# Thirty gathers, sixteen single-row loads, six comparisons and thirty-six matmuls added behind the last group of an edge kernel

## The reference, cut to what matters

```python
h = relu(layernorm(x))
p1 = tanh(h @ pp_W1 + pp_b1) @ pp_W2 + pp_b2
inter = concat([p1[src], p1[dst]], -1)
inter = ((inter @ pi_W1 + pi_b1) @ pi_W2 + pi_b2) @ pi_W3
i1 = einsum('ecb,eb->ec', inter.reshape(E, 64, 8), edge_attr_8)
i1 = tanh(i1 @ ii_W1 + ii_b1) @ ii_W2 + ii_b2
out = x + segment_sum(i1, dst, 6250)
```

## Time and profile before

| | us |
|---|---|
| median of 2 runs | 2029.59 |
| lowest, highest | 2029.33, 2029.85 |
| span of the profiled execution, first to last instruction | 2030.8 |
| granted TensorE clock, mean | 0.937 |
| TensorE busy / DVE / ACT / POOL, share of the span | 87% / 65% / 54% / 74% |

### The profile page before, as it was taken

One profiled execution on the slowest core, in us unless ns is written; L12 is line 12 of the kernel. 1 busy time (PEld: TensorE's weight loads), 2 busy tenths in 40 slices (PEclk: granted clock), 3 DMA queues, 4 the chain that ended last, 5 costly groups with the idle time before them and its releaser, 6 DMA issues.

```text
span 2030.8 us, 54857 instructions
## 1 busy us (share of the span) xinstructions
PE 1771.0 (87%) x19990; PEld 1155.3 (57%) x19990; DVE 1322.5 (65%) x1894; ACT 1100.3 (54%) x2401; POOL 1501.1 (74%) x1582
## 2 busy tenths in 40 slices
PE   7698888888888989888898889998888888888898
PEld 6465555555555555555555555555555555555665
DVE  7676666666666666666666666666656666666665
ACT  5565555555555555555555555555555555555554
POOL 2777777777777777777777777777777777777774
PEclk9799999899999899999999999988989999899999
DMA  5533233232332332323323323323233233222231
GB/s 132 126 68 61 56 60 63 54 61 54 64 61 55 62 60 55 61 55 61 61 56 61 62 57 61 61 56 60 56 60 61 57 61 59 55 58 56 57 74 42
DMA packets 261683, 126.82 MB, mean 62 GB/s; under 512 B 183546, under 2 KB 233705, under 8 KB 261433
## 3 DMA queue, kind: packets, MB, share of 16 engines
q1 hardware_dynamic: 210863, 74.12, 17.1%
q0 software_dynamic: 50048, 51.35, 14.3%
q10 hardware_dynamic: 646, 0.13, 0.0%
HBM read 119.47 MB, written 6.00 MB: 62 GB/s over the span
## 4 chain that ended last, share of the span: by engine, by line
POOL 68%; issue 22%; PE 7%; DMA 1%; DVE 1%; ACT 1%; SPq 1%; DVEq 0%; ACTq 0%; POOLq 0%
POOL u_rows L469 68%; PE bank L1162 3%; PE bank L1145 1%; PE bank L1239 1%; DMA u_rows<-u_tab,src_e 1%; PE bank L1169 0%; PE spread_ps L1154 0%; DMA x_sb<-x 0%; DVE o_sb L796 0%; PE spread_ps L1016 0%; PE bank L1137 0%; ACT loc_rows L571 0%; PE spread_ps L1004 0%; DMA v_tab<-acc_all 0%; SPq L353 0%
## 5 line engine op out<-in xcount | busy, mean ns | idle before, releaser
L469 POOL DMA_INDIRECT u_rows<-u_tab,src_e x1564 | 1494.6, 956 | 508.9 <-issue 475.2
L796 DVE TENSOR_TENSOR o_sb<-st_sb,spread_ps 128x2048 f32<-128x2048 f32 x391 | 894.1, 2287 | 484.4 <-PE spread_ps L1154 472.8
L614 ACT ACTIVATE st_sb<-bank,s_bias 64x256 f32<-64x256 f32 x1564 | 734.3, 470 | 462.5 <-PE bank L1145 446.4
L1162 PE MATMUL bank<-o_sb,g_sb 128*64 128x256 f32 x6256 | 844.3, 417 | 1.0 <-DVE o_sb L796 0.8
L1162 PEld LDWEIGHTS bank<-o_sb,g_sb 128*64 128x64 f32 x6256 | 447.6, 147 | 248.2 <-issue 61.0
L1145 PE MATMUL bank<-ident,u_rows 128*128 128x128 f32 x1564 | 287.0, 308 | 217.9 <-DMA u_rows<-u_tab,src_e 216.8
L1145 PEld LDWEIGHTS bank<-ident,u_rows 128*128 128x128 f32 x1564 | 210.3, 195 | 265.9 <-DMA u_rows<-u_tab,src_e 245.1
L1239 PEld LDWEIGHTS bank<-hot,t_sb 128*65 128x65 f32 x3128 | 222.9, 143 | 158.0 <-issue 155.8
L602 ACT ACTIVATE tt_sb<-bank,z_bias 128x256 f32<-128x256 f32 x391 | 186.1, 476 | 212.7 <-PE bank L1162 212.7
L1239 PE MATMUL bank<-hot,t_sb 128*65 128x42 f32 x3128 | 270.0, 239 | 0.5 <-ACT t_sb L605 0.5
L605 ACT COPY t_sb<-bank 128x256 f32<-128x256 f32 x391 | 146.9, 376 | 218.0 <-PE bank L1169 218.0
(11 more groups left out here) (113 smaller groups left out, 239.6 us busy)
## 6 DMA issues: line engine op xcount, KB each, us to landing
loc_bc<-loc_tab SPq DMA_DIRECT2D x391, 126.0 KB
u_rows<-u_tab,src_e POOLq DMA_INDIRECT x1564
v_win<-v_tab SPq DMA_DIRECT2D x391, 15.8 KB
basis<-edge_attr SPq DMA_DIRECT2D x24, 256.0 KB, 4.3
v_tab<-acc_all SPq DMA_DIRECT2D x6, 336.0 KB
u_tab<-basis SPq DMA_DIRECT2D x6, 224.0 KB
x_sb<-x SPq DMA_DIRECT2D x1, 1120.0 KB
out<-x_sb SPq DMA_DIRECT2D x1, 784.0 KB
```

What stands on the lines that cost most here:

```text
L469: pool.indirect_dma_start(out=u_rows[:, g % UR, j, :], out_offset=None, in_=u_tab[:, :], in_offset=bass.IndirectOffsetOnAxis(ap=src_e[:, g ...
L614: last = nc.scalar.activation(tiles[h * D:(h + 1) * D, j], s_ps[r][part].rearrange("p (q a e) -> p q a e", q=2, a=TILES), ACT.Identity, bi ...
L796: return nc.vector.tensor_tensor(o_sb[:, r, :, :].rearrange("p c (j e) -> p j c e", j=TILES), st_sb[:, r, :].rearrange("p (j e) -> p j e", ...
L1162: last = nc.tensor.matmul(z_ps[h * D:(h + 1) * D, 0:2 * P], g_sb[:, c, :], o_sb[:, r, c, 2 * h * P:(2 * h + 2) * P], start=(c == 0), stop= ...
```

## The change

Behind everything that the fast path did, each engine gets more work. Its results go to buffers that nothing reads for the output. POOL, after the last group's rows are placed, issues 30 more gathers from `u_tab`, three each of 128, 127, 126, 124, 120, 112, 96, 64, 32 and 16 rows, and waits for them. SP and ACT each, behind their stores, wait for these 30 gathers, then read eight indices from `src_e` one after the other, issue for each a load of a single row of `u_tab`, and wait for the eight. DVE, behind its last addition, copies the iota to PSUM and repeats comparisons with that operand (four of the `hot` kind and two of the `hot_t` kind). TensorE, behind `y_late`, waits for DVE and for the gathers and does three times the sum by target, six transposes and six products with the identity. Nothing is removed or moved.

```diff
+    TRIED = (128, 127, 126, 124, 120, 112, 96, 64, 32, 16)
...
@@ SP, fast path
                 store_rest()
+                sp.wait_ge(tried_u, 16 * 3 * len(TRIED))
+                for r in range(8):
+                    row = sp.value_load(src_e[0:1, r:r + 1], min_val=0, max_val=N - 1)
+                    sp.dma_start(u_rows[r:r + 1, 6, 0, :], u_tab[bass.ds(row, 1), :]).then_inc(tried_rows, 16)
+                sp.wait_ge(tried_rows, 16 * 8)
@@ POOL, fast path, behind the loop over the groups
+                pool.wait_ge(s_ready, NG)
+                at = 0
+                for rows in TRIED:
+                    for _ in range(3):
+                        pool.indirect_dma_start(
+                            out=u_rows[0:rows, at // TILES, at % TILES, :], out_offset=None, in_=u_tab[:, :],
+                            in_offset=bass.IndirectOffsetOnAxis(
+                                ap=src_e[0:rows, at:at + 1].bitcast(u32), axis=0),
+                        ).then_inc(tried_u, 16)
+                        at += 1
+                pool.wait_ge(tried_u, 16 * 3 * len(TRIED))
@@ ACT, fast path
                 store_rest()
+                act.wait_ge(tried_u, 16 * 3 * len(TRIED))
+                for r in range(8):
+                    row = act.value_load(src_e[0:1, r:r + 1], min_val=0, max_val=N - 1)
+                    act.dma_start(u_rows[r + 8:r + 9, 6, 0, :], u_tab[bass.ds(row, 1), :]).then_inc(tried_rows_a, 16)
+                act.wait_ge(tried_rows_a, 16 * 8)
@@ DVE, fast path
                 add_late()
+                iota_ps = bank[5][:, 2 * P:2 * P + W]
+                nc.vector.tensor_copy(iota_ps, iota_f[:, 0:W]).then_inc(tried_iota, 1)
+                dve.wait_ge(tried_iota, 1)
+                for g in range(4):
+                    nc.vector.tensor_tensor(
+                        hot[:, g, :, :],
+                        loc_e[:, g * TILES:(g + 1) * TILES].unsqueeze(2).to_broadcast([P, TILES, W]),
+                        iota_ps.unsqueeze(1).to_broadcast([P, TILES, W]), ALU.is_equal)
+                for g in range(2):
+                    nc.vector.tensor_tensor(hot_t[:, g % 2, :], loc_bc[0:3 * W, g, :],
+                                            iota_ps[0:3 * W, 0:1].to_broadcast([3 * W, GE]), ALU.is_equal)
+                dve.drain().then_inc(tried_add, 1)
@@ PE, fast path
                 y_late()
+                pe.wait_ge(tried_add, 1)
+                pe.wait_ge(tried_u, 16 * 3 * len(TRIED))
+                for _ in range(3):
+                    for j in range(TILES):
+                        for h in range(2):
+                            nc.tensor.matmul(bank[4][h * D:(h + 1) * D, 0:W], t_sb[:, h, j, 0:D], hot[:, h, j, :],
+                                             start=(j == 0), stop=(j == TILES - 1))
+                for _ in range(3):
+                    for q in range(2):
+                        nc.tensor.transpose(bank[4][:, q * P:(q + 1) * P],
+                                            u_rows[:, 0, 2 * q:2 * q + 2, :].rearrange("p j k -> p (j k)"), ident[:])
+                for _ in range(3):
+                    for q in range(2):
+                        last = nc.tensor.matmul(bank[4][:, q * P:(q + 1) * P],
+                                                u_rows[:, 0, 2 * q:2 * q + 2, :].rearrange("p j k -> p (j k)"),
+                                                ident[:], start=True, stop=True)
+                last.then_inc(tried_pe, 1)
+                pe.wait_ge(tried_pe, 1)
```

More of the change, by code:

```diff
@@ L259, in program @@
         x_again = sem("x_again")
+        tried_u = sem("tried_u")
+        tried_rows = sem("tried_rows")
+        tried_rows_a = sem("tried_rows_a")
+        tried_add = sem("tried_add")
+        tried_iota = sem("tried_iota")
+        tried_pe = sem("tried_pe")
         stored = sem("stored")
```

## The result

The changed kernel takes 2076.1 us (2075.54 and 2076.66) against 2029.59: a ratio of 1.0226, 95% interval 1.0209 to 1.0243, 46.5 us more. The forecast was 2068.4, 38.8 us more, and "within 2%" had the larger chance. The time is inside the range and beyond the 2% line, on the side of the dear cases.

The account below looks back on a forecast made before the run. One added chain behind the old work was taken as the bound: gathers landed at 2053.2, plus 15.7 for rows and 0.7 way out, 2069.6 against a span of 2030.8; 38.8 us on 2029.6 gave 2068.4 us, range 2061 to 2077.

Parts of the forecast that it names:

- the dear cases: Outcomes slower by more than 2%: Rival 1, Rival 4, most of Rival 2, a sixth of the forecast; together 0.41.
- What bounds the kernel, and where the added chain starts: End of the kernel: gathers released at 2015.60, first starting at 2015.75, then one chain of gathers, row loads, way out.
- Gathers at the full price: POOL's 30 added gathers: steps of 1.25 us, last start at 2052.2, landing 3.5 us later at 2055.7.
- What fewer rows are worth: POOL's smaller gathers: saving between nothing and 7.4 us; a third, 2.5 us, taken, putting the landing at 2053.2.
- Row loads: Register reads and single-row loads behind the gathers: 1.61 us a step on SP, 1.70 on ACT; 15.7 us on ACT.
- What lies beside it: TensorE's added work, 4.4 us or 8.8 at half clock, ends 6.9 us ahead of ACT's rows; DVE's 2.5 us hidden.
- The way out: Program's end behind the last landing: the last 0.7 us of the span, taken as fixed.
- The base: Span difference of 38.8 us added to the median of the runs, 2029.6, giving 2068.4 us.
- Rival 1: Row loads: a register as address makes the issue dear, 0.77 us on SP, 0.94 on ACT; 2071.6 us, chance 0.18.
- Rival 2: POOL's gathers: each costs the full 0.944 us whatever its rows; 2070.9 us, chance 0.15.
- Rival 3: POOL's gathers: time is proportional to their rows; 2063.5 us, chance 0.12.
- Rival 4: Odd row counts run on few DMA engines, POOL held until they have room, losing 5.2 us; 2076.1 us, chance 0.08.

Follow-up runs that it names:

- the run without idle time: Changed kernel with POOL waiting slot by slot instead of for the last group of all, so its 30 gathers follow at once: 2071.78 us, 1.0198 of before.
- 30 full gathers: Changed kernel with all 30 added gathers of 128 rows instead of the ten sizes: 2068.67 us, 1.0182 of before.
- the ten other sizes: Changed kernel with its gather sizes replaced by 122, 125, 121, 61, 31, 17, 100, 113, 97 and 64 rows, three each: 2088.9 us, one execution.
- the kernel with DVE's part alone: Changed kernel with only DVE's copy, six comparisons and the semaphores' declarations left: 2593.5 us against 2589.6 before on that chip, ratio 1.0013.

## Why the prediction was right or wrong

*What bounds the kernel, and where the added chain starts.* Right. The kernel's groups are untouched, the chain is gathers, rows, way out, and the run without idle time took the expected 3 us off it. The release itself came 2.4 us later in this execution. In the other runs that wait for the last placement, on such chips, the first added gather started between 2015.8 and 2021.0, while executions of before spread over 9 us by themselves. The comparison of tails and times above leaves 1 or 2 us of it for the change at the most.

*Gathers at the full price.* Right to 0.1 us, shown with 30 full gathers. Only the landing was mis-sized, 3.5 us for 2.2 to 2.5. The rows that I took had other transfers beside them, which is the likely reason; it wasn't tried.

*What fewer rows are worth.* This is the step that failed, with +8.0 us the largest error. I chose a third of a bound between 0 and 7.4 us less. Measured, the small counts that 16 divides save little: 0.91 for 64 rows, 0.84 for 16 and 0.95 for 112 against 0.944, about 0.6 us for the lot. And the uneven ones cost more: 3 x (2.55 - 0.944) = 4.8 us for 127 rows and 3 x (1.29 - 0.944) = 1.0 for 124, with 0.1 each for 126 and 120. My bounds ended at "saves nothing"; the true value was outside them, +5.5 us above the full price. The sentence of the Trainium skill that I weighed (DMA: Bandwidth & Descriptors, "Anatomy of one DMA — SWDGE (gpsimd) path"), by which many descriptors cost little, holds over 16 engines, where 112 more rows cost 0.1 us, and fails for uneven counts: the cost is 0.013 us for each row of the busiest engine, 1.6 us more for 127 rows.

*Row loads.* The mechanism was right, the size 3.8 us too high. On ACT, which ends the chain, the last issue started 10.6 us behind the landing of the gathers and not 13.1, because the register read was 0.48 us and not 0.77 (on SP 0.49, and the issue 0.26 and not 0.40). From that start to the end it was 2.0 us and not 3.3 (2.6 and 0.7): a single row is back sooner than the loads and stores that I took. I had noted the minimum of 0.464 and what it would save. Why the same read takes 0.77 in the groups wasn't tried.

*What lies beside it.* Hidden, as said, but by less than I wrote. TensorE's products took 5.6 us, where I had priced 4.4 at full clock and 8.8 at half; the pricing was wrong twice. I took 8 entries of the sum by target for all of a round, though a round has 16, and the six placements for 1.5 times instead of 3. Counted rightly, the rows give 7.5 us at full clock. What saved it is that the 48 entries took 2.79 us and not the 4.0 of the earlier trace rows, though at half the clock. The granted clock behind TensorE's 33 us of waiting was 0.50 (the lower level, 1.2 GHz) until 2066, with the products running from 2062.4, and 1.00 (2.4 GHz) from 2067; in the mean of the stretch 0.67:

```profile
2062.00:2069.00 7.00, 5.63 (x66) 5.39 (x66) 0.00 (x0) 0.00 (x0) 0.00 (x0) 0.67 0.01 3
```

The margin to ACT's end was 3.1 us instead of 6.9, because TensorE's way out takes 3.5.

*The way out.* 0.7 us fits where SP or ACT is last, and is wrong as a constant: POOL's drain took 0.55 to 8.1 us behind the added gathers, and TensorE's came 3.4 to 4.0 us behind the added products, 2.0 behind the last ones of before. What sets either wasn't tried. It cost the sum nothing, as ACT was last, but all that I would have said of the parts.

*The base.* I added the span's difference to the median, taking the profiled execution for one of the two that were timed. With 1.8 us from span to time, as every later run shows, it was one of 2032.6 us, and 15 more executions of before had medians of 2032.3 and 2032.9. The two that gave 2029.59 were quick ones. Of the 46.5 us measured, 41.7 are the tail; the rest is no more than this scatter.

*The rivals.* Rival 1 (dear issue with a register as address) is refuted, 0.26 and 0.47 us. Rival 2 (full price) nearly described the counts that 16 divides. Rival 3 (proportional) is refuted. Rival 4 gave 2076.1, the measured time to the digit, and half by accident. Its rule, the Trainium skill's on the number of engines (DMA: Bandwidth & Descriptors, "Why a DMA increments its semaphore by 16 and not by 1"), fits all 19 counts that ran: 61 and 122 rows alike, 17 above 64. Its mechanism here was wrong: POOL isn't held until the engine has room, since it is busy for its 2.56 us while the DMA engines stand idle. Its price was luck as well: the packet of 1026 bytes is a mean of 16 packets of 2048 bytes and 16 of 4 for each full gather, and 127 rows go in eight packets, not in 32. And its 5.2 us for the gathers stood beside a landing and rows that I had too dear.

*The chances.* Slower by more than 2% had 0.41 and came true, mostly through the uneven counts of rival 4, though not by its mechanism. Seen from the tail alone, 41.7 us or 2.05%, it was as close to the line as the numbers said.

## What to carry to other kernels

Give an indirect gather a row count that 16 divides, padding with a repeated index if need be (the padding itself wasn't tried): 127 rows cost POOL 2.55 us and landed after 6.1, 128 cost 0.94 and landed after 2.5. Shrinking a gather saves next to nothing, 0.1 us from 128 to 16 rows. And before a branch at the end of a program is called hidden, read the drains: the way out was 0.6 to 8.1 us on POOL and 2.0 to 4.0 on TensorE.

## What the runs showed that I had not expected

- POOL's time for a gather is 0.84 + 0.0134 us for each row of the busiest DMA engine over all counts tried, 16 to 128, within 0.05 us for nearly every gather.
- POOL's drain took 4.8 us behind gathers that ended with 16 or with 127 rows, 0.55 behind the ten other sizes (the run with the gap of 4.20 us among its gathers), and 8.1 behind 30 full ones. Whether the gap is the same work done earlier stays open. The first row is of the ten other sizes, the second of the 30 full gathers:

```profile
L77 POOLq DRAIN  x1: 552/552/552, 2074.6 to 2074.6; - x1
```

```profile
L77 POOLq DRAIN  x1: 8070/8070/8070, 2054.7 to 2054.7; - x1
```

- One chip ran the same kernel before in 2589.6 us, 28% above the others, with a mean granted clock of 0.86. In a stretch of 400 us of the kernel with DVE's part alone, against the same stretch before (second row):

```profile
1000.00:1400.00 400.00, 307.18 (x3102) 197.76 (x3100) 201.65 (x279) 165.03 (x372) 238.16 (x248) 0.85 0.22 46
```

```profile
1000.00:1400.00 400.00, 354.02 (x3986) 226.61 (x3984) 259.68 (x360) 216.67 (x477) 302.69 (x320) 0.93 0.30 59
```

There POOL waits for TensorE's placements instead of setting the pace (248 gathers in 400 us instead of 320). What slows TensorE on that chip isn't settled: the clock alone, 0.85 for 0.93, is a third of it at most.
